# A four-stage conditional block on one core: even gathers, values through DRAM by unit, values projected from x2

## The chip, the cores and the metric

The kernel runs on 1 core of one Trainium2 chip. The metric is the time of one execution on the device in microseconds (us). TensorE is called PE, VectorE DVE, ScalarE ACT, GpSimd POOL and SyncE SP.

## What is computed

The input x has 32 sequences of 32 tokens with 256 channels. Four layers follow each other, each added to its input:

```python
x = x + einsum('bct,bcd->bdt', x, W0[cond])                     # mix of the 32 tokens, by sequence
x = x + x @ W1.T + adapter(x)                                   # rank 16, one of 8 adapters by sequence
x = x + attention(x, Wq, Wk, Wv, Wo, k_blocks, v_blocks, block_tables, kv_lens)
x = x + x @ W3[id] + b3[id]                                     # one of 16 experts by sequence
```

The attention has 8 query heads and 4 key/value heads of width 32, norms and rotations on queries and keys, and a window of 128 keys. Keys and values of the past lie in blocks of 16 rows. Each sequence first writes its 32 new keys and values into the pools at the blocks that its table names. Block tables may name one block several times, and in several sequences, so a written row can be seen through any of them.

## The kernel before

Below, x1 is the result of the first layer and x2 that of the second. Everything is float32. The sequences stand in three units of 11, 11 and 10. Each sequence sees at most 11 blocks in its window, so a unit is a tile `blkp[u]` of 121 or 110 partitions, one block each, with keys and values of 16 rows side by side. A fourth set of 96 blocks (index `NU`) holds the blocks that are written.

The order of the work is written out by hand: each engine has one instruction list, and semaphores join them. An engine that waits holds everything behind it in its list.

- **Front.** PE turns the weights, composes keys and values with layer 1 (`W1` plus the identity, times `Wk` and `Wv`), mixes the tokens (`mix_down`, L970), makes x1, projects keys and values from x1 (`project_kv`, L990) and runs layer 1 (L1003) to x2, from which it projects the queries (L1017). The composed weights let keys and values start before x2 exists.
- **Gathers.** POOL gathers table entries (L442) and then the blocks: 8 indirect DMAs (L449), each with one row of 8 KB for each of 96, 121 or 110 partitions, in the order writers, unit 0, unit 1, unit 2. ACT or DVE rearrange each from its raw place (`permute`, L562 and L809) into `blkp`. The gathers of unit 2 reuse the raw space of the writers' blocks.
- **Rows of the writes.** A chain on PE, DVE and POOL works out which written row each new row replaces: PE selects (L1182), POOL shifts (L476), DVE writes `row_i` (L900).
- **Scatter and patch.** The writers' blocks go to DRAM (L356). POOL scatters the new keys and values over them by 8 indirect DMAs (L499), the first four after the first half of keys and values is ready, the others after the second. When all have landed, three indirect DMAs (L507) fetch the blocks that were written over `blkp[0]`, `blkp[1]` and `blkp[2]`: the patches.
- **Values.** After the patch SP moves the values of each sequence from `blkp` into the shape that PE needs, 128 rows into `Vm` (L376) and 48 into `Vt` (L377), two DMAs for a sequence, 64 in all:

```python
sp.dma_start(Vm[:, b, :], by_o[u][main:main + BP, :, 1, :]).then_inc(s_v[b // B4], 16)
sp.dma_start(Vt[lo:lo + KB, b // 2, b % 2, :], by_o[u][tail:tail + BT_, :, 1, :]).then_inc(s_v[b // B4], 16)
```

- **Experts.** Then SP loads expert weights (L391, 256 KB each), 16 ahead and 16 in the loop. They lie in the space of `blkp[0]` and `blkp[2]`, so they need its keys turned and its values moved. The biases (L516, POOL) lie in `blkp[1]`.
- **Loop.** PE turns the keys (L1048) and queries, then walks over 16 pairs of sequences: scores (L1067), DVE adds the mask and takes the maximum (L933), ACT exponentiates (L680), POOL normalises (L522), PE turns the probabilities (L1079) and multiplies the values (L1102). After each group of four sequences PE projects (L1115) and runs layer 3 (L1128), and SP writes the result (L402). A group is two pairs, and there are 8 groups.

## Time and profile before

| | |
|---|---|
| median of 3 runs | 203.7 us (203.66 to 204.32) |
| the profiled execution's own time | 204.03 us |
| its span | 202.2 us, 3950 instructions |
| PE busy | 125.5 us (62%) |
| ACT busy | 88.2 us (44%) |
| DVE busy | 72.7 us (36%) |
| POOL busy | 67.9 us (34%) |
| DMA | 30.51 MB, mean 151 GB/s |

The span runs from the first to the last instruction of the profiled execution; the time around it (1.8 us) is not in the profile. Times in the rows below are us from the start of the span. The chain of waits is followed back from the last instruction: at each step to what released it. PEclk is the clock that PE was granted as a share of the full 2.4 GHz, and the DMA share is the mean busy share of the core's 16 DMA engines.

### The profile page before, as it was taken

To read this page: it belongs to the slowest core of one execution; us is meant where nothing else is said; L and a number is where in the kernel's file an instruction comes from. 1 tells how busy PE (TensorE), PEld (TensorE's weight loads), DVE (VectorE), ACT (ScalarE), POOL (GpSimd) and SP (SyncE) were. 2 spreads that over 40 slices of the span, in tenths; PEclk is the share of its full clock that TensorE was granted. 3 is DMA by queue.
4 is the path that set the end of the run, shared out by engine and by line. 5 is a ranking of instruction groups with operands and counts; after the bars stand their busy time and mean duration, and the time that the engine had idled before them with its cause. 6 is when DMAs were issued, how large, how long until landed. Compare 5 with 4: busy or idle time off the path is not lost.

```text
span 202.2 us, 3950 instructions
## 1 busy us (share of the span) xinstructions
PE 125.5 (62%) x1400; PEld 94.0 (46%) x1400; DVE 72.7 (36%) x307; ACT 88.2 (44%) x244; POOL 67.9 (34%) x83
## 2 busy tenths in 40 slices
PE   0229899994039830086689700070399999999883
PEld 0129759961037320084557500050167777677571
DVE  0794445556501775002444410000033435335211
ACT  2130392737565740045979700050027567656410
POOL 4577433170067714100025000680017425224300
PEclk9999999999556996559999975555579999999999
DMA  4937999999993692994333333444777887750000
GB/s 124 313 33 218 243 177 164 138 349 245 169 195 117 176 234 61 208 150 105 66 61 65 64 61 57 100 121 118 226 242 246 255 244 200 227 164 18 29 29 26
DMA packets 25675, 30.51 MB, mean 151 GB/s; under 512 B 6585, under 2 KB 23741, under 8 KB 24398
## 3 DMA queue, kind: packets, MB, share of 16 engines
q1 hardware_dynamic: 22392, 17.96, 34.1%
q0 software_dynamic: 2848, 11.77, 28.3%
q10 hardware_dynamic: 416, 0.54, 0.8%
q8 instruction: 11, 0.18, 0.4%
q14 instruction: 8, 0.07, 0.1%
HBM read 26.91 MB, written 4.03 MB: 153 GB/s over the span
## 4 chain that ended last, share of the span: by engine, by line
DMA 29%; SPq 25%; PE 21%; issue 10%; POOL 8%; DVE 4%; ACT 1%; POOLq 1%; DVEq 0%
DMA vt_m<-in_L_cond_v_blocks,tab_i 17%; SPq L377 13%; SPq L376 10%; DMA blkp<-wr_rows,patch_i 5%; PE bank L1067 4%; PE bank L1128 4%; PE bank L1115 3%; DMA wr_rows<-kvn_m,row_i 3%; POOL wr_rows L499 3%; PE bank L1079 3%; DMA lens_i<-in_itok_B 2%; POOL tab_i L442 2%; PE bank L1123 2%; PE bank L1102 2%; DMA blkp<-in_L_cond_W 1%
## 5 line engine op out<-in xcount | busy, mean ns | idle before, releaser
L522 POOL TENSOR_TENSOR xin_m<-xin_m,ri 128x704 f32<-128x704 f32 x16 | 21.8, 1361 | 62.2 <-DVE ri L925 62.2
L680 ACT ACTIVATE xin_m<-kvn_m,nb 128x176 f32<-128x176 f32 x64 | 27.5, 435 | 5.6 <-DVE nb L933 5.6
L690 ACT COPY x_m<-bank 128x512 f32<-128x512 f32 x16 | 9.4, 589 | 44.5 <-PE bank L1079 44.5
L1067 PE MATMUL bank<-kt_m,natQ 32*64 32x176 f32 x256 | 20.7, 331 | 4.0 <-DVE nb L933 2.7
L1079 PE MATMUL bank<-cst,xin_m 128*128 128x128 f32 x64 | 11.0, 299 | 16.8 <-POOL xin_m L522 16.6
L933 DVE CUSTOM_DVE_ANT_0 kvn_m<-bank,mask 128x176 f32<-128x176 f32 x64 | 17.5, 329 | 3.6 <-PE bank L1067 3.6
L942 DVE TENSOR_TENSOR wq_m<-bank,blkp 128x256 f32<-128x256 f32 x8 | 3.4, 425 | 42.8 <-PE bank L1128 42.8
L1017 PE MATMUL bank<-wq_m,x_m 128*128 128x256 f32 x32 | 10.2, 482 | 12.4 <-ACT x_m L605 11.1
L1067 PEld LDWEIGHTS bank<-kt_m,natQ 32*64 32x64 f32 x256 | 12.6, 136 | 10.7 <-DVE nb L933 5.3
L1048 PE MATMUL bank<-cst,blkp 121*128 121x121 f32 (+1 forms) x48 | 7.3, 317 | 15.9 <-DMA blkp<-wr_rows,patch_i 15.5
L1079 PEld LDWEIGHTS bank<-cst,xin_m 128*128 128x128 f32 x64 | 7.6, 150 | 19.7 <-POOL xin_m L522 17.8
L1128 PE MATMUL bank<-blkp,wkv_m 128*32 128x256 f32 x128 | 9.6, 416 | 9.9 <-DMA blkp<-in_L_cond_W 9.9
L1017 PEld LDWEIGHTS bank<-wq_m,x_m 128*128 128x128 f32 x32 | 7.8, 254 | 15.5 <-ACT x_m L605 11.9
L1048 PEld LDWEIGHTS bank<-cst,blkp 121*128 121x128 f32 (+1 forms) x48 | 6.3, 169 | 17.0 <-DMA blkp<-wr_rows,patch_i 16.3
L516 POOL DMA_INDIRECT blkp<-in_L_cond_b,eid_i x8 | 7.9, 986 | 18.2 <-DMA vt_m<-blkp 16.9
L869 DVE TENSOR_REDUCE ssq<-ksq 128x16 f32<-128x512 f32 x4 | 2.7, 686 | 28.4 <-ACT ksq L588 16.4
L680 ACT ACTIVATION_READ_ACCUMULATOR xin_m<-kvn_m,nb 128x1 f32 x64 | 12.3, 192 | 0.0
L612 ACT COPY kt_m<-bank 128x484 f32<-128x484 f32 (+1 forms) x12 | 5.9, 569 | 13.1 <-PE bank L1048 13.1
L990 PE MATMUL bank<-wkv_m,x_m 128*128 128x128 f32 x64 | 10.1, 280 | 0.0
L1115 PE MATMUL bank<-w_m,WoT 128*128 128x128 f32 x64 | 9.3, 288 | 1.1 <-DVE w_m L920 1.1
L1128 PEld LDWEIGHTS bank<-blkp,wkv_m 128*32 128x32 f32 x128 | 4.0, 115 | 12.4 <-DMA blkp<-in_L_cond_W 10.2
L1115 PEld LDWEIGHTS bank<-w_m,WoT 128*128 128x128 f32 x64 | 7.7, 191 | 2.9 <-issue 1.5
(192 smaller groups left out, 274.6 us busy)
## 6 DMA issues: line engine op xcount, KB each, us to landing
blkp<-in_L_cond_W SPq DMA_DIRECT2D x32, 256.0 KB, 3.4
vm_m<-blkp SPq DMA_DIRECT2D x32, 64.0 KB
wr_rows<-blkp SPq DMA_DIRECT2D x1, 1536.0 KB, 16.2
mask<-mask_rows SPq DMA_DIRECT2D x4, 352.0 KB
xin_m<-in_x SPq DMA_DIRECT2D x2, 512.0 KB
out<-wq_m SPq DMA_DIRECT2D x8, 128.0 KB, 3.1
vt_m<-blkp SPq DMA_DIRECT2D x32, 24.0 KB
mask_rows<-m SPq DMA_DIRECT2D x4, 88.0 KB
```

Source lines behind the costliest of these rows:

```text
L376: sp.dma_start(Vm[:, b, :], by_o[u][main:main + BP, :, 1, :]).then_inc(s_v[b // B4], 16)
L377: sp.dma_start(Vt[lo:lo + KB, b // 2, b % 2, :], by_o[u][tail:tail + BT_, :, 1, :]).then_inc(s_v[b // B4], 16)
L522: pool.tensor_tensor(e_, e_, ri[:, p % 2, :].unsqueeze(2).broadcast_to([P, 4, KEYS]), ALU.mult).then_inc(s_pn, 1)
L680: act.activation(pr_seq(n % 2, u, j), S[:, n % 2, u, j, :], ACT.Exp, bias=nb[:, n % 2, 2 * u + j:2 * u + j + 1], scale=-1.0, accum_out=rs[ ...
L933: dve.tensor_tensor_reduce(S[:, n % 2, u, j, :], bank[2 + (2 * n + u) % 3][:, j * KEYS:(j + 1) * KEYS], mask[:, 2 * n + j, :], -SCALE, 3e3 ...
L990: mm(o, x1T[:, kc, tile], WkvT[:, kc, w], start=(kc == 0), stop=False)
L1017: i_ = mm(o, x2T[:, kc, t * P:(t + 1) * P], WqT[:, kc, :, :].rearrange("p s c -> p (s c)"), start=(kc == 0), stop=(kc == KC - 1))
L1048: i_ = tr(bank[KT_BANK[c % 4]][:, o * P:o * P + PU[u]], by_o[u][0:PU[u], 4 * (c % 4) + o, 0, :], ident[0:PU[u], 0:PU[u]])
L1067: i_ = mm(bank[2 + i % 3][GS * T * k:GS * T * k + GS * T, j * KEYS:(j + 1) * KEYS], QT[h, b // B4, b % B4, :], KT[h, b, :], start=True, st ...
L1079: i_ = tr(bank[5 + p % 2][:, (2 * j + u) * P:(2 * j + u + 1) * P], pr_main(p % 2, u, j), ident)
L1115: i_ = mm(bank[7][:, oc * P:(oc + 1) * P], WoT[:, s, oc * P:(oc + 1) * P], oT[:, g % 2, :, s, :], start=(s == 0), stop=(s == GS - 1))
L1128: i_ = mm(o[T * j:T * j + T, :], x3T[:, g % 2, kc, T * j:T * j + T], We(b)[:, kc, :], start=False, stop=(kc == KC - 1), skip_group_check=True)
```

## The change

- All gathers of the three units, and the patches, take 128 partitions. The additional table entries are read but used by nobody; the patch index of the additional rows is set so that they fetch nothing.
- The values of a unit are stored to a DRAM tensor `v_rows` by one DMA (2048 pieces of 512 B) and read back by four (two for `Vm`, two for `Vt`; even and odd sequences apart). SP does store 0, loads 0, store 1, experts 0 to 3, loads 1, store 2, experts 4 to 7, loads 2, experts 8 to 15. The experts of a space wait for the unit's store instead of its 22 copies.
- Only keys are projected from x1 by composed weights. Values are projected from x2 by plain `Wv`, kept in a new tile `WvT`.
- The composing, and the turning of `W1`, `A1` and `B1`, stand ahead of the mixing on PE; the adapter weights are loaded ahead of x. DVE adds the identity first, and does the selection of offsets and the tables after the angles; three of the eight mixing copies are ACT's instead of four.
- Both writers' blocks are rearranged on DVE, in raw space `vt_m`, which POOL then zeroes before the gathers of unit 2 (in the raw space of unit 0). The zeroing used to stand after unit 1, ahead of the scatters.
- ACT does layer 1's copies of x2 ahead of the rearranging of unit 1, and the two copies of values only after x2.
- The scores of a pair wait once and signal once, by sequence outside and half inside.
- `dist` moves out of x2's space, so that x2 no longer waits for the masks; the first query copy does.

```diff
-            for b in range(B):
-                u = UNIT_OF[b]
-                q = WB * (b - SEQS[0] * u)
-                if q == 0:
-                    sp.wait_ge(s_patch[u], 16)
-                main, tail, lo = (q + BT_, q, KB) if b % 2 else (q, q + BP, 0)
-                sp.dma_start(Vm[:, b, :], by_o[u][main:main + BP, :, 1, :]).then_inc(s_v[b // B4], 16)
-                sp.dma_start(Vt[lo:lo + KB, b // 2, b % 2, :], by_o[u][tail:tail + BT_, :, 1, :]).then_inc(s_v[b // B4], 16)
...
-                        moved(sp, u)
+                        sp.wait_ge(s_vo[u], 16)
...
+            def values_out(u):
+                sp.wait_ge(s_patch[u], 16)
+                sp.dma_start(v_rows[u].rearrange("(p o) c -> p o c", o=BLOCK), by_o[u][:, :, 1, :]).then_inc(s_vo[u], 16)
+
+            def values_back(u):
+                sp.wait_ge(s_vo[u], 16)
+                if u == 0:
+                    sp.wait_ge(s_vz, 1)
+                    for i in ((2, 0), (2, 1)):
+                        sp.wait_ge(s_perm[i], 1)
+                b0, b1 = SEQS[0] * u, SEQS[0] * u + SEQS[u]
+                src = v_rows[u][0:PU[u] * BLOCK, :].rearrange("(b r) c -> r b c", r=KEYS)
+                for i in range(2):
+                    b = b0 + (b0 + i) % 2
+                    main, tail, lo = (KB, 0, KB) if i else (0, P, 0)
+                    sp.dma_start(Vm[:, b:b1:2, :], src[main:main + P, b - b0::2, :]).then_inc(s_v[u], 16)
+                    sp.dma_start(Vt[lo:lo + KB, b // 2:(b1 - 1 - i) // 2 + 1, i, :], src[tail:tail + KB, b - b0::2, :]).then_inc(s_v[u], 16)
...
             def load_blocks(i):
                 u, kv = i
-                n = PU[u] if u < NU else NWI
+                n = P if u < NU else NWI
...
+            pool.memset(vt_m[:, :], 0.0).then_inc(s_vz, 1)
+            for kv in range(2):
+                pool.wait_ge(s_perm[0, kv], 1)
                 load_blocks((2, kv))
...
-                pool.indirect_dma_start(out=blkp[u][0:PU[u], :], out_offset=None, in_=wr_blocks,
-                                        in_offset=bass.IndirectOffsetOnAxis(ap=patch_i[0:PU[u], u:u + 1], axis=0),
+                pool.indirect_dma_start(out=blkp[u][:, :], out_offset=None, in_=wr_blocks,
+                                        in_offset=bass.IndirectOffsetOnAxis(ap=patch_i[:, u:u + 1], axis=0),
...
             permute((0, 0))
             keep_k(0)
+            act.wait_ge(s_ids, 16)
+            act.copy(idf[:, :], ids_i[:, :]).then_inc(s_idf, 1)
             root_k(0)
...
+            def project_v(i):
+                pe.wait_ge(s_x2, 2 * i + 2)
+                for t in range(4):
+                    o = bank[3 + i][:, t * KV:t * KV + KV]
+                    tile = slice((4 * i + t) * P, (4 * i + t + 1) * P)
+                    for kc in range(KC):
+                        i_ = mm(o, x2T[:, kc, tile], WvT[:, kc, :], start=(kc == 0), stop=(kc == KC - 1))
+                i_.then_inc(s_vp, 1)
...
-                for u in range(2):
-                    i = 2 * p + u
-                    if i >= 3:
-                        pe.wait_ge(s_mx, 2 * (i - 2))
-                    for j in range(2):
-                        b = 2 * p + j
+                if p:
+                    pe.wait_ge(s_mx, 4 * p - 2)
+                for j in range(2):
+                    b = 2 * p + j
+                    for u in range(2):
```

What the change moves stands in the instruction lists. SP, before, from the mask loads to the first expert (`vm_m` is the space of `Vm`, `vt_m` of `Vt`; a name in brackets is a semaphore waited for):

```order
L364 DMA mask<-mask_rows 32x5632 x3
L376 DMA vm_m<-blkp 128x1x128 [waits blocks_permuted20,blocks_permuted21,blocks_permuted31,patched0,blocks_permuted30,v_tails_zeroed]
L377 DMA vt_m<-blkp 48x1x128
...
L390 TENSOR_LOAD ids_i [waits v_moved1,v_moved0,v_moved2,k_turned,ids_loaded]
L390 ISA x2
L391 ISA
L391 DMA blkp<-in_L_cond_W 128x2x256
```

SP, after, the same place:

```order
L362 DMA mask<-mask_rows 32x5632 x3
L382 DMA v_rows<-blkp 2048x1x128 [waits patched0,ids_loaded]
L395 DMA vm_m<-v_rows 128x6x128 [waits blocks_permuted20,blocks_permuted21,v_tails_zeroed,values_out0]
L396 DMA vt_m<-v_rows 48x6x128
L395 DMA vm_m<-v_rows 128x5x128
L396 DMA vt_m<-v_rows 48x5x128
L382 DMA v_rows<-blkp 2048x1x128 [waits patched1]
L375 TENSOR_LOAD ids_i [waits values_out0,k_turned]
L375 ISA x2
L376 ISA
L376 DMA blkp<-in_L_cond_W 128x2x256
```

Between the mask loads and the first expert 64 DMAs stood before; now 6 stand there.

ACT, before, from the root of the second key half (L576) to the copies of x2 (L605); L562 rearranges a gather, L572 copies values, L642 makes distances:

```order
L576 ACTIVATE rstdk<-ssk,eps 128x16 [waits k_sums_ready]
L572 COPY kvn_m<-bank 128x4x128 [waits v_projected]
L642 ACTIVATE x_m<-cst,mid 128x176 x4
L562 COPY blkp<-vt_m 121x4x16x32 [waits blocks_loaded10]
L572 COPY kvn_m<-bank 128x4x128 [waits v_projected]
L562 COPY blkp<-vt_m 121x4x16x32 [waits blocks_loaded11]
L647 COPY WoT<-bank 128x512 [waits wo_turned]
L605 COPY x_m<-bank 128x512 [waits token_masks_ready,layer1_done]
L605 COPY x_m<-bank 128x512 [waits layer1_done]
```

ACT, after (L587 root, L627 distances, L616 x2, L573 rearranging, L583 values):

```order
L587 ACTIVATE rstdk<-ssk,eps 128x16 [waits k_sums_ready]
L627 ACTIVATE qn_m<-cst,mid 128x176 x5
L652 COPY WoT<-bank 128x512 [waits wo_turned]
L616 COPY x_m<-bank 128x512 [waits layer1_done] x2
L573 COPY blkp<-kt_m 128x4x16x32 [waits blocks_loaded10]
L583 COPY kvn_m<-bank 128x4x128 [waits v_projected]
L616 COPY x_m<-bank 128x512 [waits layer1_done] x2
L573 COPY blkp<-kt_m 128x4x16x32 [waits blocks_loaded11]
L583 COPY kvn_m<-bank 128x4x128 [waits v_projected]
```

Both copies of values now stand behind copies of x2; before, x2 stood behind both.

PE, after, from the turning of Wo (L1195) to the second projection of values (L1005); L1017 and L1018 are layer 1, L1201 selects the rows:

```order
L1195 MATMUL bank<-cst,qn_m 128x128 [waits w1_kept,wo_permuted]
L1195 MATMUL bank<-cst,qn_m 128x128 x3
L1017 MATMUL bank<-x_m,w_m 128x512 [waits lora_kept,w1_kept]
L1017 MATMUL bank<-x_m,w_m 128x512
L1018 MATMUL bank<-xaT,BT 128x512
L1201 MATMUL bank<-wr,cst 32x16 [waits patch_index_ready,rows_valued]
L1201 MATMUL bank<-wr,cst 32x16 x2
L1017 MATMUL bank<-x_m,w_m 128x512 x2
L1018 MATMUL bank<-xaT,BT 128x512
L1005 MATMUL bank<-WvT,x_m 128x128 [waits x2_kept]
L1005 MATMUL bank<-WvT,x_m 128x128 x7
```

The row selection stood ahead of Wo and of layer 1 before; it now stands behind both, and the projection of values waits for the copies of x2.

## Rows read from the trace of the kernel before

**Rows 1.** Chain of waits, in order of time: start us, us, what.

```profile
20.23 35.09 DMA vt_m<-in_L_cond_v_blocks,tab_i
...
70.43 6.44 DMA wr_rows<-kvn_m,row_i
...
77.75 9.13 DMA blkp<-wr_rows,patch_i
86.95 0.66 SPq L376
...
136.28 0.76 SPq L377
...
145.03 1.96 PE bank L1128 x16
...
155.10 1.02 PE bank L1128 x16
...
163.19 1.02 PE bank L1128 x16
```

**Rows 2.** Timeline of PE: start us, us, line, operation, count [idle before].

```profile
42.33 1.88 PE L1003 MATMUL bank<-x_m,w_m 128*128 128x512 f32 x4
...
58.76 6.24 PE L1017 MATMUL bank<-wq_m,x_m 128*128 128x256 f32 x16 [11.12 <-ACT x_m L605]
...
114.22 1.16 PE L1115 MATMUL bank<-w_m,WoT 128*128 128x128 f32 x8
...
152.06 1.16 PE L1115 MATMUL bank<-w_m,WoT 128*128 128x128 f32 x8
...
155.03 1.09 PE L1128 MATMUL bank<-blkp,wkv_m 128*32 128x256 f32 x16
156.05 0.84 PE L1067 MATMUL bank<-kt_m,natQ 32*64 32x176 f32 x16
...
159.41 0.81 PE L1067 MATMUL bank<-kt_m,natQ 32*64 32x176 f32 x8 [0.38 <-DVE nb L933]
```

**Rows 3.** Timeline of SP's DMA queue, same columns.

```profile
4.89 2.56 SPq L343 DMA_DIRECT2D natB<-in_L_cond_Bm  x2
...
138.41 17.75 SPq L391 DMA_DIRECT2D blkp<-in_L_cond_W  x16
```

**Rows 4.** Windows: stretch, length, busy of five engines, PEclk, DMA share, GB/s.

```profile
18.00:24.00 6.00, 5.23 (x29) 4.51 (x28) 3.75 (x14) 0.89 (x3) 4.03 (x8) 1.00 1.06 269
26.00:40.00 14.00, 14.00 (x111) 12.01 (x110) 7.22 (x29) 8.93 (x16) 3.74 (x9) 1.00 1.03 160
...
78.00:86.00 8.00, 0.00 (x0) 0.00 (x0) 0.76 (x2) 0.00 (x0) 3.14 (x3) 0.50 0.77 162
...
101.00:114.00 13.00, 11.88 (x186) 8.72 (x186) 6.25 (x45) 11.19 (x46) 4.07 (x3) 1.00 0.36 63
```

**Rows 5.** Timeline of ACT, front part.

```profile
27.60 0.27 ACT L626 CAST idf<-ids_i 128x32 f32<-128x32 int32 x1
...
35.78 1.90 ACT L562 COPY blkp<-kt_m 121x2048 f32<-121x2048 f32 x1 [4.29 <-DMA kt_m<-in_L_cond_k_blocks,tab_i]
...
48.61 1.44 ACT L642 ACTIVATE x_m<-cst,mid 128x176 f32<-128x176 f32 x4
...
57.63 1.08 ACT L605 COPY x_m<-bank 128x512 f32<-128x512 f32 x2
```

**Rows 6.** Timeline of POOL, front part.

```profile
28.98 0.74 POOL L463 COPY qn_m<-natQ 128x256 f32<-128x256 f32 x2 [0.19 <-POOL eid L428]
...
39.62 0.26 POOL L476 TENSOR_TENSOR rows<-rows 32x40 f32<-32x40 f32 x1 [6.30 <-DVE rows L894]
...
57.36 3.51 POOL L490 MEMSET vt_m<- 128x4096 f32 x1 [12.32 <-ACT blkp L562]
61.04 1.09 POOL L499 DMA_INDIRECT wr_rows<-kvn_m,row_i  x1 [0.17 <-issue]
```

**Rows 7.** Timeline of DVE, the row numbers (four writes, last ends 46.10).

```profile
45.36 0.74 DVE L900 TENSOR_SCALAR row_i<-rowT 32x8 int32<-32x8 f32 x4
```

More of the change, by code:

```diff
@@ L322, in program @@
         out_rows = out.rearrange("b t d -> (b t) d").rearrange("(n p) d -> n p d", p=P)
-        def moved(engine, u):
-            for g in range(SEQS[0] * u // B4, (SEQS[0] * u + SEQS[u] - 1) // B4 + 1):
-                engine.wait_ge(s_v[g], 16 * 2 * B4)
         block = ctx.enter_context(nc.Block())
@@ L392, in expert @@
                     .then_inc(s_we[b % NE // B4], 16)
-            for b in range(NE):
+            def values_out(u):
[14 more added lines that the diff above has]
+                    sp.dma_start(Vt[lo:lo + KB, b // 2:(b1 - 1 - i) // 2 + 1, i, :], src[tail:tail + KB, b - b0::2, :]).then_inc(s_v[u], 16)
+            values_out(0)
+            values_back(0)
+            values_out(1)
+            for b in range(4):
+                expert(b)
+            values_back(1)
+            values_out(2)
+            for b in range(4, 8):
+                expert(b)
+            values_back(2)
+            for b in range(8, NE):
                 expert(b)
@@ L736, in _ @@
             dve.sem_inc(s_len, 1)
+            dve.wait_ge(s_w1, 16)
+            dve.wait_ge(s_cst, 16)
+            for oc in range(KC):
+                w_ = nat[:, oc, 0, oc * P:(oc + 1) * P]
+                tt(w_, w_, ident, ALU.add).then_inc(s_w1i, 1)
+            dve.wait_ge(s_mixg, 16)
+            step(ts(mixg[:, 0:T * T:T + 1], mixg[:, 0:T * T:T + 1], 1.0, None, ALU.add))
+            dve.transpose(xaT[0:T, :], mixg.rearrange("b (c d) -> b d c", c=T)).then_inc(s_mixt, 1)
+            dve.wait_ge(s_mixt, 1)
+            dve.wait_ge(s_mixz, 1)
+            for h, q in MIX_DVE:
+                cp(*mix_part(h, q)).then_inc(s_mix, 1)
+            dve.wait_ge(s_adp, 32)
+            step(cp(amask[:, :], adp_i[:, :]))
+            ts(amask[:, :], amask[:, :], C("adapter"), scal[:, 0:1], ALU.is_equal, ALU.mult).then_inc(s_am, 1)
+            dve.wait_ge(s_an, 1)
+            side(cp(ang[:, :, 1, :], ang[:, :, 0, :]))
+            side(ts(turns[:, :, 0, :], ang[:, :, 0, :], float(1 / (2 * np.pi)), ROUND, ALU.mult, ALU.add))
+            step(ts(turns[:, :, 1, :], ang[:, :, 0, :], float(1 / (2 * np.pi)), 0.25, ALU.mult, ALU.add))
+            step(ts(turns[:, :, 1, :], turns[:, :, 1, :], ROUND, None, ALU.add))
+            step(ts(turns[:, :, :, :], turns[:, :, :, :], ROUND, None, ALU.subtract))
+            as_rows = lambda t: t[:, :, :, :].rearrange("p n k e -> p (n k e)")
+            for c in (TWO_PI_HI, TWO_PI_MID, TWO_PI_LO):
+                step(stt(as_rows(ang), as_rows(turns), -float(c), as_rows(ang), ALU.mult, ALU.add))
+            step(ts(ang[:, :, 1, :], ang[:, :, 1, :], float(np.pi / 2), None, ALU.add))
+            ts(ang[:, :, :, :], ang[:, :, :, :], PI_SAFE, -PI_SAFE, ALU.min, ALU.max).then_inc(s_ar, 1)
             side(tt(sel[0:NWI, 0, :], slot[0:NWI, 2, :], C("wr_seq", NWI), ALU.mult))
-            dve.wait_ge(s_cst, 16)
             settle()
@@ L837, in _ @@
             rotations(1)
+            side(dve.memset(found[:, 0, :], 0.0))
             dve.wait_ge(s_tgt, 1)
@@ L844, in _ @@
             settle()
-            for u in range(NU):
-                side(ts(found[0:PU[u], 1, u:u + 1], found[0:PU[u], 0, u:u + 1], 0.0, float(NONE), ALU.is_equal, ALU.mult))
-            settle()
-            for u in range(NU):
-                side(stt(patch_i[0:PU[u], u:u + 1], found[0:PU[u], 0, u:u + 1], -1.0, found[0:PU[u], 1, u:u + 1], ALU.add, ALU.add))
-            settle()
+            step(ts(found[:, 1, :], found[:, 0, :], 0.0, float(NONE), ALU.is_equal, ALU.mult))
+            step(stt(patch_i[:, :], found[:, 0, :], -1.0, found[:, 1, :], ALU.add, ALU.add))
             dve.sem_inc(s_pidx, 1)
@@ L1134, in _ @@
             turn_square(0, nat, 2).then_inc(s_kvT, 1)
+            pe.wait_ge(s_w1i, KC)
+            pe.wait_ge(s_kvTk, 2)
+            for dc in range(KC):
+                for oc in range(KC):
+                    mm(bank[1][:, dc * D:dc * D + KV], nat[:, oc, 0, dc * P:(dc + 1) * P], WkvT[:, oc, 0:KV], start=(oc == 0), stop=(oc == KC - 1))
+            turn_square(0, nat, 0).then_inc(s_w1T, 1)
             pe.wait_ge(s_ab, 16)
@@ L1192, in _ @@
             layer1(0)
+            pe.wait_ge(s_val, 1)
+            pe.wait_ge(s_pidx, 1)
+            for w in range(NW):
+                i_ = mm(bank[7][0:B, w * BLOCK:(w + 1) * BLOCK], C("wr_sel", NWI, w * B, (w + 1) * B), wr[:, 3, 0:BLOCK], start=True, stop=True)
+            i_.then_inc(s_sel, 1)
             layer1(1)
-            project_q(0)
-            project_q(1)
+            project_v(0)
             layer1(2)
             layer1(3)
-            project_q(2)
+            project_v(1)
+            for i in range(3):
+                project_q(i)
             for c in range(4):
```

197 lines of the change are left out of this document (74 added, 123 removed).

## The prediction

> **What bounds the kernel now.** The chain of waits comes first, since the busy shares average over stages with different limits. Its last third is a steady loop, and before the loop stand one gather and one queue [rows 1]. Piece by piece: the gather issued at 20.23 lands 35.09 us later; the new rows are scattered, the last landing takes 6.44 us; the patch of unit 0 takes 9.13 us and lands at 86.95. From there to 137.04 the chain holds nothing but SP issuing the 64 small copies of values (the first and the last stand in the rows; 50.1 us, 0.78 us each). Only behind them do the experts load, and layer 3 of group 0 starts at 145.03. The chain is thus front (to 86.95), SP (58.1 us) and loop (57.1 us from 145.03 to the end of the span at 202.2).
>
> The timeline of PE says what the SP part hides [rows 2]. The loop had begun: its first output projection ran at 114.22, and in the running loop layer 3 (155.03) follows the projection (152.06) by 2.97 us. Unblocked, layer 3 of group 0 would have started at 117.2, which is 30.2 us after the patch. PE waited for experts and values, not for arithmetic.
>
> **The change part by part.**
>
> *Values by unit (the copies).* 64 issues go; 3 stores and 12 loads come, and the experts 0 to 3 stand behind the first store, the four loads of unit 0 and the second store. Durations do not exist in this trace for the new pieces, so I bound them. Issue: two loads of 1024 pieces each took SP 2.56 us [rows 3], so a store of 2048 pieces costs about 2.6 us and four loads about 3. Transfer: while 512 B pieces of values moved, the rate was 63 GB/s at a DMA share of 0.36 [rows 4], hence 63/0.36 = 175 GB/s if the engines were kept full; 1.05 MB takes 6 us at that rate and 17 us at the bare 63 GB/s. I take 175, since share 0.36 says that SP was the limit. With P the time at which patch 0 lands and some 2 us for a landing (an estimate; the experts took about 3 us in all): store 0 lands at P+10, the loads of unit 0 at P+19, store 1 at P+21, experts 0 to 3 (1.1 us of issue each: 16 in 17.75 us [rows 3]) at P+23. The first product with values came at P+22.3 and layer 3 needs its experts at P+30.2. Experts 4 to 7, behind store 2, land at about P+34 (needed at P+38), 8 to 15 at P+40 to P+47 (8 to 11 needed at P+46). All are covered, by 3 to 7 us; if that cover is gone, the excess is paid one for one. POOL's bias gathers wait for store 1 in front of the fourth normalisation: P+21 against P+24, covered too. So the 58.1 us shrink to 30.2: **27.9 us gained**.
>
> *A warm TensorE.* Layer 3 of group 0 to that of group 1 took 10.07 us, the next such step 8.09 [rows 1]: after the idle stretch PE ran at the granted 0.50, that is 1.2 GHz, which also shows as 0.50 in the wait for the patch [rows 4]. Without that stretch the step should be a normal one: **2.0 us gained**.
>
> *Scores in one group.* In steps with nothing between, PE already runs all 16 score records in 0.84 us; in the others the second half starts at 159.41 after a wait of 0.38 us for DVE [rows 2]. The new order waits for the same two reductions before all 16. Start 159.4 plus 0.8 is 160.2, and the next instruction began at 160.15. Zero.
>
> *The front (when the patch lands).* Removed from PE are the value projections from x1 with their adapter part and half of each composed product; the composing moves ahead of the mixing. This makes x1 some 5 us earlier, but three things keep that from reaching the patch. I follow the new order instruction by instruction.
> The keys of unit 0 (the third gather of blocks) landed at 35.78, where ACT stopped waiting for them [rows 5]. Gathers went at 269 GB/s while the 96-row ones moved (18 to 24 us) and at 160 GB/s in 26 to 40 us, DMA share 1.03 to 1.06 both times [rows 4]. So full engines moved 40% less with 121 rows. At 269 GB/s the keys of unit 0, 1.05 MB behind the 1.57 MB of the 96-row gathers, which I let begin at 17.5 us (an estimate), land at 27.3; unchanged, at 35.8. I take 29, near the rate of the even gathers.
> Then ACT: rearrange 1.9, two copies 1.1, ids to float 0.3 (now behind the keys; before at 27.60) gives 32.3. POOL: from the ids to the end of the Wo copies 1.85 us, 34.1 [rows 5, 6]. Behind that on POOL: the zeroing of the tails 3.5 and two gather issues at 1.3 (the eight scatters from 61.04 to 70.43 are 1.34 apart [rows 1, 6]), 40.2. PE turns Wo (0.6, estimate), runs layer 1 pass 0 (4 of its 6 records 1.88, so 2.7 us [rows 2]) and selects the rows at 37.8, in time. The row chain took 39.62 to 46.10 [rows 6, 7], 6.5 us: 46.7. The moved selection and tables on DVE are paid ahead of this and hidden by the gather.
> Now the new knot: ACT's root of the second key half needs DVE's sum, which stands behind the row chain: 47.7 with 1 us for both (estimate by the 0.5 us of a 128x512 copy). Behind it on ACT: five distances 1.8 [rows 5], Wo 0.6, two copies of x2 1.1: 51.2. Values now need x2, so PE starts their first projection here, after 10 us of idling: 16 records, 1.9 us by layer 1's columns, 3.1 by the 6.24 us of the 256-wide ones at the low clock [rows 2]; 2.6 gives 53.8. Layer 1 passes 2 and 3: 59.2. Copy of x2, rearranging, copy of values 3.0: 62.2. Scatters 5 to 8 start here, the last at 66.2. Its landing: 6.44 before, with the mask load in flight, which now is over; 3 us for an expert load; I take 4.5, 70.7. Patch: issue 0.8, then 9.13 us before with 121 rows; the DMA share meanwhile was 0.77 [rows 4], and with full engines it would be 7.0; I take 8. P = 79.5, against 86.95: **7.5 us gained**.
>
> *Rule against row.* [Rows 4] show no idle engines at 121 rows, only slower ones, so from rows alone the even gather could gain nothing or all of the 40%. The Trainium skill, "DMA: Bandwidth & Descriptors", section on why a DMA increments its semaphore by 16, says that a transfer is spread over the largest number up to 16 that divides its slowest dimension: 121 rows would use 11 engines, 128 use 16, and a row would be taken by 8 instead of 11 turns of an engine. By that page alone, the stretch from 23.3 us (the end of the 96-row gathers at 269 GB/s) to 35.8 would shrink by 8/11 to 9.1 us; the keys would land at 32.4, and the sum would be 3.4 us longer. That page's count of engines is not visible in the profile.
>
> *Sum.* The profiled execution took 204.03 us (span 202.2 and 1.8 around it); 204.03 - 27.9 - 2.0 - 7.5 = **166.6 us**. The median of the runs is 203.7, 0.3 below that execution, so the same gains from there give 166.3.
>
> **The rivals.**
> 1. *Gathers stay slow.* The keys of unit 0 land at 35.8, everything behind them shifts by 6.8, and P is 86.3: 173.4 us. For: the DMA share was already over 1.0. Against: 269 GB/s with 96 rows.
> 2. *Values come back late.* At 100 GB/s store 0 lands at P+14, and loads 0 with store 1 (2.0 MB) need 20 us more: the first product with values slips from P+22.3 to P+34, 12 us: about 178. For: patches 1 and 2, experts and values share the queue's engines. Against: the 175 GB/s above.
> 3. *The round trip through DRAM is the new bound, and the kernel is slower.* If pieces of 512 B move at the 63 GB/s that the window shows, each store or load takes 17 us; store 0, then loads 0 with store 1, loads 1 with store 2, loads 2 add up to 99, and experts 8 to 11 arrive at about P+104. From layer 3 of group 2 to the end are 57.1 - 2.0 - 16.2 = 39 us: 79.5 + 104 + 39 + 1.8 = 224. It beats the old time only if those experts come by P+83, that is above some 78 GB/s. Against: DMA share 0.36 at 63 GB/s.
> 4. *The front is faster than I make it*, for instance because the scatters land within 3 us and the patch in 6, and the passes of layer 1 run ahead of my ACT estimate: P about 70, 157 us.
>
> **How the numbers follow.** Chances: the sum with its own spread (159 to 173) 0.58; rival 1 0.16; rival 2 0.11; rival 3 0.04; rival 4 0.11. P's bounds are 74 (landing 3.4, patch 5.5, projections warm) and 89 (keys at 35.8, landing 6.4, patch 9.1), so 161 to 176 from the front alone, and 12 more from late values. The range 155 to 182 leaves out rival 3, the ends of rival 2 and the far side of rival 4, and should hold 8 in 10. A difference of 0.3% is about what a measurement of this kernel can tell from no change: only rival 3 reaches that far, so faster 0.95, same 0.01, slower 0.04.
>
> **What would show it.** Right: SP's first store within 1 us of patch 0 and 15 DMAs of values in all; layer 3 of group 0 some 30 us after patch 0, no PE gap over 5 us from then on, steps of 8.1 us from the first; gathers above 200 GB/s between 26 and 40 us; on ACT a wait for the sum of the second key half near 46, and the last scatter issue at 66. Wrong: a patch that lands outside 74 to 89, PE waiting for the values loaded back or for the expert weights by more than 3 us, or a loop step other than 8.1.

## The result, and the profile after

The changed kernel took 168.2 us (median of 4 runs, 166.62 to 169.18), the kernel before 204.0 on the same chip (4 runs, 203.66 to 205.33): a ratio of 0.821, 95% interval 0.813 to 0.829. The forecast was 166.6 us. The profiled execution took 166.62 us with a span of 164.8, against 204.03 and 202.2 before.

The span falls into the same three pieces as in the prediction:

| | before | forecast | after |
|---|---|---|---|
| front, until patch 0 lands (P) | 86.95 | 79.5 | 76.3 |
| P to layer 3 of group 0 | 58.1 | 30.2 | 32.5 |
| from there to the end | 57.1 | 55.1 | 56.0 |
| span | 202.2 | 164.8 | 164.8 |

The chain of waits of the kernel after, in order of time (start us, us, what), answers to [rows 1]:

```profile
16.13 10.43 DMA vm_m<-in_L_cond_k_blocks,tab_i
...
49.16 3.71 PE bank L1005 x16
...
66.03 2.55 DMA wr_rows<-kvn_m,row_i
69.38 6.92 DMA blkp<-wr_rows,patch_i
76.34 3.49 PE bank L1062 x16
...
107.35 4.68 DMA blkp<-in_L_cond_b,eid_i
```

SP has left the chain. The gather that begins it is the keys of unit 0, 10.4 us, and a value projection (L1005) is a link now. The timeline of PE (start us, us, line, operation, count [idle before]), to be read beside [rows 2]:

```profile
95.02 1.45 PE L1080 MATMUL bank<-kt_m,natQ 32*64 32x176 f32 x16 [0.49 <-DVE nb L940]
...
105.12 0.83 PE L1080 MATMUL bank<-kt_m,natQ 32*64 32x176 f32 x16 [1.26 <-DVE nb L940]
...
108.84 1.09 PE L1142 MATMUL bank<-blkp,wkv_m 128*32 128x256 f32 x16
...
117.34 1.09 PE L1142 MATMUL bank<-blkp,wkv_m 128*32 128x256 f32 x16
121.80 0.83 PE L1080 MATMUL bank<-kt_m,natQ 32*64 32x176 f32 x16 [1.22 <-DVE nb L940]
125.52 1.09 PE L1142 MATMUL bank<-blkp,wkv_m 128*32 128x256 f32 x16
```

Layer 3 of group 0 waits for no expert. The first step from layer 3 to layer 3 is 8.50 us and the next four are 8.18; the last two, 6.58 and 4.38, are as before. Inside the first step DVE waits for the biases of layer 3:

```profile
112.14 0.42 DVE L949 TENSOR_TENSOR wq_m<-bank,blkp 128x256 f32<-128x256 f32 x1 [3.54 <-DMA blkp<-in_L_cond_b,eid_i]
```

The timeline of SP's queue, beside [rows 3]:

```profile
76.36 0.57 SPq L382 DMA_DIRECT2D v_rows<-blkp  x1
87.39 0.38 SPq L395 DMA_DIRECT2D vm_m<-v_rows  x1
...
89.47 0.55 SPq L382 DMA_DIRECT2D v_rows<-blkp  x1
91.33 6.41 SPq L376 DMA_DIRECT2D blkp<-in_L_cond_W  x4
97.79 0.47 SPq L395 DMA_DIRECT2D vm_m<-v_rows  x1
```

Store 0 leaves at P, and the loads that wait for it go 11.0 us later (forecast 10). Windows of the kernel after (stretch, length, busy of five engines, PEclk, DMA share, GB/s), beside [rows 4]:

```profile
26.00:40.00 14.00, 11.76 (x73) 8.11 (x71) 9.56 (x26) 7.04 (x11) 7.47 (x10) 1.00 0.96 381
86.40:96.40 10.00, 7.70 (x73) 5.88 (x73) 3.34 (x20) 7.46 (x26) 1.35 (x1) 0.69 0.84 228
96.40:106.40 10.00, 8.73 (x142) 6.75 (x139) 3.92 (x28) 8.56 (x35) 6.38 (x6) 0.80 1.01 274
```

All transfers together move 381 GB/s in the stretch in which they moved 160 before. Besides the gathers, the store of the writers' blocks (`wr_rows`, 1.5 MB) is in flight in both. Last, the timelines of ACT, POOL and DVE in the front, beside [rows 5 to 7]:

```profile
26.58 1.90 ACT L573 COPY blkp<-vm_m 128x2048 f32<-128x2048 f32 x1 [3.10 <-DMA vm_m<-in_L_cond_k_blocks,tab_i]
...
45.71 0.31 ACT L587 ACTIVATE rstdk<-ssk,eps 128x16 f32<-128x16 f32 x1 [5.74 <-DVE ssk L876]
...
60.78 0.58 ACT L583 COPY kvn_m<-bank 128x512 f32<-128x512 f32 x1 [0.34 <-PE bank L1005]
```
```profile
31.33 3.50 POOL L481 MEMSET vt_m<- 128x4096 f32 x1
...
39.47 0.29 POOL L493 TENSOR_TENSOR rows<-rows 32x40 f32<-32x40 f32 x1
...
54.41 1.07 POOL L507 DMA_INDIRECT wr_rows<-kvn_m,row_i  x1 [10.51 <-ACT kvn_m L583]
```
```profile
32.11 2.75 DVE L856 TENSOR_SCALAR found<-found 128x3 f32<-128x3 f32 x1
...
44.22 0.74 DVE L907 TENSOR_SCALAR row_i<-rowT 32x8 int32<-32x8 f32 x4
```

Two things to see: POOL waited 10.5 us for the values that now come from x2, and a DVE instruction over 3 elements a partition took 2.75 us while POOL zeroed `vt_m`.

### The profile page after: what moved, and what is told of

Read it like the earlier page. It is cut to its first block, busy times and chain, and to the rows that moved or that the text cites. A ratio compares the mean times of both kernels' runs of the same rounds, so it can differ in the third digit from the quotient of the medians.

```text
span 164.8 us, 3872 instructions
## 1 busy us (share of the span) xinstructions
PE 116.0 (70%) x1384; PEld 89.3 (54%) x1384; DVE 76.2 (46%) x306; ACT 86.6 (53%) x243; POOL 67.1 (41%) x83
## 4 chain that ended last, share of the span: by engine, by line
PE 40%; DMA 17%; POOL 13%; issue 11%; ACT 8%; DVE 7%; POOLq 1%; SPq 0%; DVEq 0%
PE bank L1080 7%; DMA vm_m<-in_L_cond_k_blocks,tab_i 6%; PE bank L1092 4%; DMA blkp<-wr_rows,patch_i 4%; PE bank L1129 4%; PE bank L1062 4%; PE bank L1142 4%; PE bank L1005 4%; DMA blkp<-in_L_cond_b,eid_i 3%; PE bank L1116 3%; DMA lens_i<-in_itok_B 2%; PE bank L1137 2%; POOL tab_i L456 2%; POOL vt_m L481 2%; PE bank L1017 2%
## 5 line engine op out<-in xcount | busy, mean ns | idle before, releaser
L530 POOL TENSOR_TENSOR xin_m<-xin_m,ri 128x704 f32<-128x704 f32 x16 | 21.8, 1360 | 49.8 <-DVE ri L932 49.8
L1080 PE MATMUL bank<-kt_m,natQ 32*64 32x176 f32 x256 | 14.5, 343 | 10.0 <-DVE nb L940 9.1
L1080 PEld LDWEIGHTS bank<-kt_m,natQ 32*64 32x64 f32 x256 | 9.0, 141 | 14.4 <-issue 14.2
L1062 PEld LDWEIGHTS bank<-cst,blkp 121*128 121x128 f32 (+1 forms) x48 | 7.4, 191 | 13.4 <-DMA blkp<-wr_rows,patch_i 10.5
L507 POOL DMA_INDIRECT wr_rows<-kvn_m,row_i x8 | 8.0, 1006 | 15.2 <-ACT kvn_m L583 13.4
L1005 PE MATMUL bank<-WvT,x_m 128*128 128x128 f32 x32 | 5.8, 354 | 11.5 <-ACT x_m L616 11.5
L1005 PEld LDWEIGHTS bank<-WvT,x_m 128*128 128x128 f32 x32 | 5.3, 261 | 13.1 <-ACT x_m L616 13.1
L573 ACT COPY blkp<-vm_m 128x2048 f32<-128x2048 f32 x4 | 7.6, 1892 | 3.1 <-DMA vm_m<-in_L_cond_k_blocks,tab_i 3.1
L955 DVE TENSOR_TENSOR wkv_m<-bank,x_m 128x256 f32<-128x256 f32 x8 | 3.4, 425 | 11.9 <-PE bank L1129 11.9
L1142 PE MATMUL bank<-blkp,wkv_m 128*32 128x256 f32 x128 | 8.7, 385 | 0.0
L1116 PE MATMUL bank<-x_m,vm_m 128*32 128x64 f32 x256 | 8.7, 225 | 0.0
## 6 DMA issues: line engine op xcount, KB each, us to landing
wr_rows<-blkp SPq DMA_DIRECT2D x1, 1536.0 KB, 10.5
```

The costliest lines, as they stand in the source:

```text
L507: pool.indirect_dma_start(out=wr_rows, out_offset=bass.IndirectOffsetOnAxis(ap=row_i[:, n:n + 1], axis=0), in_=kvn[:, n, :], in_offset=Non ...
L530: pool.tensor_tensor(e_, e_, ri[:, p % 2, :].unsqueeze(2).broadcast_to([P, 4, KEYS]), ALU.mult).then_inc(s_pn, 1)
L1005: i_ = mm(o, x2T[:, kc, tile], WvT[:, kc, :], start=(kc == 0), stop=(kc == KC - 1))
L1062: i_ = tr(bank[KT_BANK[c % 4]][:, o * P:o * P + PU[u]], by_o[u][0:PU[u], 4 * (c % 4) + o, 0, :], ident[0:PU[u], 0:PU[u]])
L1080: i_ = mm(bank[2 + (2 * p + u) % 3][GS * T * k:GS * T * k + GS * T, j * KEYS:(j + 1) * KEYS], QT[h, b // B4, b % B4, :], KT[h, b, :], star ...
L1116: mm(o, Vm[:, b, v], PTA[:, p % 2, j, k // 2, c], start=True, stop=False)
```

## Experiments: the parts of the change

The runs came in three batches, each beside the kernel before: the four of this section (before 202.4 us, 11 runs), the first four of the next (203.8, 7 runs) and the last three (204.0, 6 runs). Ratios are to the kernel before on the same chip, with 95% intervals.

Each trace is of one execution, and the start of the front alone moves by 2 us between them: in the changed kernel and in five kernels below that have the same gathers up to there (scores by half, the two late zeroings and the two with x2 first), the keys of unit 0 land between 26.58 and 28.62. So a P that differs by less than 2 us shows nothing by itself; where it matters, P is counted below from the landing of the keys (49.8 us in the changed kernel, 50.4 in the kernel with scores by half, whose front is the same).

**Values by unit alone, on the kernel before.**

```diff
-                sp.dma_start(Vm[:, b, :], by_o[u][main:main + BP, :, 1, :]).then_inc(s_v[b // B4], 16)
...
+                sp.dma_start(v_rows[u][0:PU[u] * BLOCK, :].rearrange("(p o) c -> p o c", o=BLOCK), by_o[u][0:PU[u], :, 1, :]).then_inc(s_vo[u], 16)
...
-                pe.wait_ge(s_v[p // 2], 16 * 2 * B4)
+                pe.wait_ge(s_v[UNIT_OF[2 * p]], 64)
+                pe.wait_ge(s_v[UNIT_OF[2 * p + 1]], 64)
```

> The kernel before with the values by unit through DRAM and nothing else of the change. Theory (the 64 copies on SP held the experts back): patch 0 stays at 87, layer 3 of group 0 runs 30 to 33 us behind it instead of 58, the next step is warm: 204.0 - 27.9 - 2.0 = 174, up to 176 if the round trip costs as much as in the changed kernel. Rival (the change's gain is mostly the front, and unit-wise values only pay with even gathers): above 185.

Measured: 177.2 us, ratio 0.872 (0.865 to 0.878), span 176.5. PE's timeline:

```profile
87.25 3.49 PE L1060 MATMUL bank<-cst,blkp 121*128 121x121 f32 x16 [12.72 <-DMA blkp<-wr_rows,patch_i]
...
118.24 1.09 PE L1141 MATMUL bank<-blkp,wkv_m 128*32 128x256 f32 x16
...
128.45 1.09 PE L1141 MATMUL bank<-blkp,wkv_m 128*32 128x256 f32 x16 [0.46 <-DMA blkp<-in_L_cond_W]
```

From P to layer 3 it is 31.0 us against 58.1, as expected. This part carries 25.7 of the 37.4 us by which the span fell. The time is above the 174 to 176 expected, and the next step was not the short one: it took 10.2 us, although no stretch with an idle PE stands ahead of it. There DVE waited 4.83 us for the biases of layer 3, and the expert weights came 0.46 us late.

**Everything but that part.** The changed kernel, with the 64 copies put back.

```diff
-            values_out(0)
-            values_back(0)
...
+                sp.dma_start(Vm[:, b, :], by_o[u][main:main + BP, :, 1, :]).then_inc(s_v[b // B4], 16)
+                sp.dma_start(Vt[lo:lo + KB, b // 2, b % 2, :], by_o[u][tail:tail + BT_, :, 1, :]).then_inc(s_v[b // B4], 16)
```

> The changed kernel with the values moved by 64 copies as before. Theory (the parts add): patch 0 at 76.3, then 58.1 us to layer 3 of group 0, 57.1 from there, 1.8 around: 193. Rival (with the front shortened, copies and patches collide): above 197, or below 190 if the copies issue faster behind even patches.

Measured: 195.9 us, 0.967 (0.960 to 0.973), span 194.0. This is 2.9 us above the 193 expected. P is at 78.48, 2.1 us later than in the changed kernel, so most of the gain in front of it is kept; but SP's copies again hold layer 3 back, 58.0 us after P:

```profile
136.47 1.96 PE L1130 MATMUL bank<-blkp,wkv_m 128*32 128x256 f32 x16 [10.38 <-DMA blkp<-in_L_cond_W]
```

The two parts save 25.7 and 8.2 us of span by themselves and 37.4 together. They add, nearly. Of the 3.5 over, 2.4 lie in P and 2.7 behind layer 3 of group 0, above all in two long steps (10.2 and 9.0 us) of the kernel with only the values by unit; 1.6 go the other way, since there layer 3 followed P after 31.0 us and not 32.5.

**Gathers, patches and stores of 121 and 110 rows in the changed kernel.**

```diff
-                n = P if u < NU else NWI
+                n = PU[u] if u < NU else NWI
...
-                pool.indirect_dma_start(out=blkp[u][:, :], out_offset=None, in_=wr_blocks,
+                pool.indirect_dma_start(out=blkp[u][0:PU[u], :], out_offset=None, in_=wr_blocks,
```

> The changed kernel with gathers, patches and stores of 121, 121 and 110 partitions. Theory (the rate of the gathers is set by the count of partitions, and the front waits for the keys of unit 0): gathers fall from 381 to about 170 GB/s in 26 to 40 us, the keys of unit 0 land at 31 to 36 instead of 26.6, patch 0 moves by 4 to 9 us: 172 to 177. Rival (the order of ACT hides the gathers, the rate comes from the raw spaces or from the earlier start): same rate, or within 1.5 us of the changed kernel.

Measured: 180.4 us, 0.887 (0.879 to 0.895), span 178.1: 12 us more than the changed kernel, 13 by the ratios. Window, ACT and chain:

```profile
26.00:40.00 14.00, 5.10 (x43) 4.82 (x43) 4.88 (x23) 3.30 (x5) 2.17 (x6) 0.79 1.01 245
```
```profile
34.42 1.90 ACT L573 COPY blkp<-vm_m 121x2048 f32<-121x2048 f32 x1 [12.60 <-DMA vm_m<-in_L_cond_k_blocks,tab_i]
```
```profile
78.08 9.66 DMA blkp<-wr_rows,patch_i
```

The keys of unit 0 come 7.8 us later (34.42 against 26.58), the patch takes 2.7 us longer (9.66 against 6.92), and P moves by 11.4 to 87.8. So the row count alone is worth as much as the whole front gained, 10.6 us: without it, P is within 1 us of where it was before.
**Scores by half again.**

```diff
-                i_.then_inc(s_sc, 1)
+                    i_.then_inc(s_sc, 1)
...
-                    dve.wait_ge(s_sc, n + 1)
+                        dve.wait_ge(s_sc, 2 * n + u + 1)
```

> The changed kernel with the waits and the order of the scores of before. Theory (regrouping is neutral, as predicted): within 0.5 us. Rival (one wait for both halves makes PE wait 1.2 us for DVE once a group instead of 0.4, a step of 8.18 against 8.08): 0.7 to 1.5 us faster than the changed kernel.

Measured (6 runs): 169.1 us, 0.828 (0.822 to 0.834), span 167.6. In the steady loop PE's wait falls from 1.22 us to 0.39 and the step from 8.18 to 8.09:

```profile
132.93 0.81 PE L1081 MATMUL bank<-kt_m,natQ 32*64 32x176 f32 x8 [0.39 <-DVE nb L940]
136.65 1.09 PE L1143 MATMUL bank<-blkp,wkv_m 128*32 128x256 f32 x16
```

Over the four full steps that is 0.4 us, less than runs of one kernel differ. The time does not tell the two apart, the steady step does. The first step took 10.25 us here against 8.50, which is 1.75 us of the 2.8 by which this span is longer; this edit does not touch what it waited for, see the end of the next section.

## Experiments: what the front still waits for

**Zeroing of vt_m behind the row numbers.** POOL's memset moved from before the last two gathers to 44 us.

```diff
-            pool.memset(vt_m[:, :], 0.0).then_inc(s_vz, 1)
...
             pool.sem_inc(s_rowf, 1)
+            pool.memset(vt_m[:, :], 0.0).then_inc(s_vz, 1)
```

> The changed kernel with POOL's zeroing of the tails behind the row chain instead of ahead of the gathers of unit 2. Theory (the 3.5 us memset stands on the front's chain twice: it delays the gathers of unit 2, and a 3-element DVE instruction takes 2.75 us beside it and holds the sum that ACT's root waits for): that DVE instruction takes 0.3 us, the row chain starts at 36.5 instead of 39.5, patch 0 moves from 76.3 to 73.4: about 165. Rival (the DVE instruction is slow for another reason and POOL has slack): patch 0 within 1 us of 76.3.

Measured: 169.7 us, 0.839 (0.830 to 0.848): not faster. DVE and POOL tell why:

```profile
34.22 0.22 DVE L856 TENSOR_SCALAR found<-found 128x3 f32<-128x3 f32 x1
...
44.30 3.95 DVE L907 TENSOR_SCALAR row_i<-rowT 32x8 int32<-32x8 f32 x4
```
```profile
44.14 3.51 POOL L498 MEMSET vt_m<- 128x4096 f32 x1 [0.15 <-POOL rows L494]
```

The 2.75 us were due to the zeroing, as thought: without it beside them they are 0.22. But the zeroing takes the delay along: the row numbers beside it take 3.95 us in place of 0.74. In these two instructions the edit gave 2.5 us and took 3.2. P is 79.5; of the 3.2 us by which it is later, 1.9 were there when the keys landed (28.47).

**Copies of x2 ahead of the key root on ACT.**

```diff
             keep_k(1)
-            root_k(1)
...
             keep_x2(0)
             keep_x2(1)
...
+            root_k(1)
             keep_v(0)
```

> The changed kernel with ACT's first two copies of x2, Wo and the rearranging of unit 1's keys ahead of the root of the second key half, and the distances later. Theory (ACT's order, not PE, DMA or POOL, sets the front: ACT sits 5.7 us at the root while the finished x2 waits behind it): values of the second half are kept near 52 instead of 61.4, patch 0 lands at 67 to 69; ACT's query work then ends near 70 and takes back 1 to 3 us: 160 to 162. Rival (the gathers or the row chain bind right behind it): patch 0 at 73 or later.

Measured: 166.5 us, 0.813 (0.798 to 0.829), span 161.7 in the profiled execution; the interval does not part it from the changed kernel. P was to land at 67 to 69 and the time to be 160 to 162; P is 72.3. The last scatter is issued 8.4 us earlier, P comes only 4.0 earlier. The chain:

```profile
57.63 6.63 DMA wr_rows<-kvn_m,row_i
64.32 0.54 issue
65.06 7.19 DMA blkp<-wr_rows,patch_i
```

The landing takes 6.6 us in place of 2.55. The window masks, 1.4 MB which SP had started at 57.09, are in flight in those microseconds; in the changed kernel they started at 54.51, 11.5 us ahead of the last scatter. The edit itself moved them back, since it puts the last distances, from which the masks are made, behind the copies of x2.

**Both of these.**

> The zeroing late and x2 first together, on the changed kernel. Theory: the row chain ends 3 us earlier, but the last scatter then hangs on layer 1 and ACT, so the two overlap: patch 0 at 66 to 68, 157 to 161. Rival (they are one and the same delay): the same as x2 first alone within 0.5 us.

Measured: 167.9 us, 0.829 (0.817 to 0.840), span 165.3, not the 157 to 161 that the sum of the two would give. The row numbers take 3.95 us, and the last landing 8.46:

```profile
60.15 8.46 DMA wr_rows<-kvn_m,row_i
69.40 6.95 DMA blkp<-wr_rows,patch_i
```

**Values projected from x1 again**, with the composed weights, in the changed kernel. Two moves of order come with it: PE projects both halves ahead of layer 1's second half, and ACT keeps both halves ahead of the second key root, where the kernel before kept them behind it.

```diff
-                        i_ = mm(o, x2T[:, kc, tile], WvT[:, kc, :], start=(kc == 0), stop=(kc == KC - 1))
+                        mm(o, x1T[:, kc, tile], WkvT[:, kc, KV:2 * KV], start=(kc == 0), stop=False)
+                    i_ = mm(o, xaT[:, tile], BKV[:, KV:2 * KV], start=False, stop=True)
```

> The changed kernel with the values projected from x1 by composed weights again, right behind layer 1's first half, and kept by ACT ahead of the root of the second key half. Theory (projecting from x2 put layer 1 and two copies of x2 in front of the scatters and cost the front more than the 3 us of PE work it saved): last scatter issue near 54, patch 0 at 64 to 68, 159 to 163. Rival (the saved PE work is worth more, since the row selection stands on PE): patch 0 at 76 or later, 168 or more.

Measured: 162.4 us, 0.795 (0.783 to 0.806), span 158.7: faster than the change. By the ratios it is 5.4 us, and an estimate from the two intervals puts that within 3 us either way; the runs scattered from 160.5 to 164.9. How much of it is the source of the values and how much the new places on ACT and PE was not tried apart. The scatters start at 45.72, 8.7 us earlier, and P is 68.2. The landing is slow again:

```profile
55.72 4.50 DMA wr_rows<-kvn_m,row_i
61.01 7.14 DMA blkp<-wr_rows,patch_i
```

**The same with the masks early.** ACT's five distances go ahead of `keep_v`, DVE's mask ahead of the transposition of the row numbers.

```diff
+            dve.wait_ge(s_dist, NT)
+            ts(m4_own[:, :, :], dist, (WINDOW / 2) ** 2, -BIG, ALU.is_ge, ALU.mult).then_inc(s_m4, 1)
             dve.wait_ge(s_rowf, 1)
```

> The kernel whose values come from x1 again (run e7), with the window masks made and spread earlier: ScalarE's last five distances before it keeps the values, VectorE's mask built before the row numbers are transposed. Theory (the 1.4 MB of mask loads, 56.06 to 61.99 in that run, share the DMA engines with the last scatters, 52 to 56.7, and hold their landing back: 4.32 us waited behind the last issue, where the changed kernel with its masks out by 60.5 and its last scatter issued at 66.03 waited 2.23): mask loads near 50 to 56, the wait for the last landing 2 to 2.5 us, patches 1 to 2 us earlier, span 156.5 to 158. Rival 1 (the landing is the scatters' own, 512 kB in rows of 512 B, whatever else is loaded): wait 4 to 5, span 158 to 159.5. Rival 2 (the queries behind, not the patches, bound the next step): patches earlier, span unchanged.

Measured: 158.6 us, 0.776 (0.769 to 0.784), span 157.7. SP's queue and the chain:

```profile
47.16 2.92 SPq L361 DMA_DIRECT2D mask<-mask_rows  x4
```
```profile
56.18 2.40 DMA wr_rows<-kvn_m,row_i
59.38 6.93 DMA blkp<-wr_rows,patch_i
```

The landing is 2.4 us again, so the masks had held it back, and P is 66.4. The theory holds. The median moved by more (3.8 us) than P (1.8); the two were not run side by side, and their intervals touch. Counted from the keys, P came after 41.7 us there and 39.7 here. The span of the profiled execution fell by only 1.0, since its first step was longer (10.75 us against 10.41).

**Zeroing last, alone and on top of the masks.** The memset stands behind the three patches.

```diff
+            pool.memset(vt_m[:, :], 0.0).then_inc(s_vz, 1)
             pool.wait_ge(s_eidi, 1)
```

> The changed kernel with GpSimd's zeroing of vt_m (3.5 us) moved behind the patches' issue at 72. Theory (a VectorE instruction that reads one tensor and a scalar can't run beside that zeroing: found<-found took 2.75 us beside it, and 0.22 with the zeroing moved to 44, where the row numbers then took 3.95 us in place of 0.74): both short again, found 0.2 and row numbers 0.7; second patched half of unit 0 waits less; patch 0 at 74.5 to 76, span 163 to 165, unless one of the recips or copies of the query rotation (VectorE from 64 on) stalls in their place, which would show as a long instruction at 72 to 76. Rival (the 2.75 us is a wait for something else, such as the matmul before): found stays long, span 164.8.

Measured: 168.1 us, 0.819 (0.810 to 0.828): no gain, where P was to land at 74.5 to 76. It landed at 78.3, which counted from the keys (28.62) is 49.7 us, as in the changed kernel. Yet both DVE groups are short now:

```profile
36.01 0.17 DVE L856 TENSOR_SCALAR found<-found 128x3 f32<-128x3 f32 x1
...
46.09 0.74 DVE L907 TENSOR_SCALAR row_i<-rowT 32x8 int32<-32x8 f32 x4
```

What ate the gain stands in front of them in this execution: PE waited 2.35 us for DVE's `hit` and then ran part of the key projection at the low clock (1.06 us for four records in place of 0.61), so `found` started 7.4 us behind the keys and not 5.5. One trace cannot say whether the edit brings that about.

> Both edits (masks early, zeroing last) on the kernel with values from x1. If both theories hold and add: row numbers done 0.5 to 1.5 us earlier, wait for the last landing 2 to 2.5 us, patch 0 at 64.5 to 66.5 (68.2 without them), span 155 to 157. Rival (queries bound the step after the patches): patch 0 as early, span 157.5 to 158.7.

Measured: 156.4 us (155.71 to 157.6), 0.769 (0.763 to 0.776), span 154.0: the fastest of all, 11.8 us below the change in the medians. The chain:

```profile
54.86 2.41 DMA wr_rows<-kvn_m,row_i
...
58.07 6.75 DMA blkp<-wr_rows,patch_i
64.86 3.49 PE bank L1060 x16
```

P is 64.9, 1.5 us earlier than with the masks alone (37.6 us behind the keys, against 39.7). The intervals of these two overlap, so of this last step only the rows speak. And they say that P is the smaller part: the span fell by 3.7 us, and 2.6 of them are the first step, 8.18 us here and 10.75 there. Two spans alone must not be read as the worth of the late zeroing.

**What makes the first step long.** In it DVE waits for four bias gathers (L524 in the changed kernel), which POOL issues between its normalisations. Sorted by that wait, in all kernels with values by unit and scores in one group:

| kernel | wait of DVE | first step |
|---|---|---|
| zeroing late | 2.94 | 8.18 |
| masks and zeroing last | 2.97 | 8.18 |
| zeroing last | 3.15 | 8.17 |
| x2 first | 3.26 | 8.22 |
| both late zeroing and x2 first | 3.42 | 8.37 |
| changed kernel | 3.54 | 8.50 |
| values from x1 | 3.84 | 10.41 |
| masks early | 4.23 | 10.75 |
| odd gathers | 4.76 | 11.31 |

From 3.26 us on the step grows with the wait, and between 3.54 and 3.84 it jumps by 1.9 us (scores by half, with 3.80 us, took 10.25). Behind the wait PE ran at different clocks. With masks early, then in the changed kernel:

```profile
103.49 0.42 DVE L947 TENSOR_TENSOR wq_m<-bank,blkp 128x256 f32<-128x256 f32 x1 [4.23 <-DMA blkp<-in_L_cond_b,eid_i]
...
104.90:110.20 5.30, 5.22 (x66) 4.44 (x66) 1.98 (x14) 3.43 (x15) 3.90 (x4) 0.68 1.13 279
```
```profile
113.60:117.30 3.70, 3.68 (x66) 3.12 (x66) 1.92 (x14) 2.75 (x13) 2.94 (x3) 1.00 1.14 284
```

The same 66 records of PE took 5.2 us at a granted 0.68 and 3.7 at 1.00. The granted clock behind the wait is 0.67 or 0.68 in the last three kernels of the table and with scores by half, and 1.00 in the six above. So 1.5 of the 1.9 us of the jump are a slower PE, and 0.3 us more of waiting go with 2 us of span. The kernel before with the values by unit stands apart: 4.83 us, a first step of 10.21, and the clock stayed at 1.00. This is read from the traces; a kernel whose biases come early was not run.

## Why the prediction was right, and where it was off

The forecast, 166.6, is the time of the profiled execution (166.62) and 1.6 us below the median. Three misses cancel in the first: -3.2, +2.3 and +0.9 us of span. That the span comes out at 164.8, as forecast, is luck; the pieces are right to 1, 2 and 3 us.

- **Values by unit: right in mechanism, 2.3 us too good.** Forecast -27.9, in the trace 58.1 to 32.5 = -25.6, alone 58.1 to 31.0. Store 0 landed at P+11 (forecast P+10), experts 0 to 3 went out from P+15 to P+21. Nothing waited for values. In the store two misses cancel as well: SP issued it in 0.57 us, not 2.6, and the rest took 10.5 us, not 8. The step that failed is "unblocked, layer 3 would have started 30.2 us after the patch", which took over the pace of the kernel before. There PE was granted 1.00 from 97 to 107 us (P+10 to P+20), here 0.69 in the same stretch behind P, and 0.80 in the next where it was 1.00 before: part of the score groups ran at 1.2 GHz (1.45 us for 16 records in place of 0.83). And the last scores ahead of the projection waited 1.26 us for DVE, not 0.38. In the kernel before with the values by unit, the clock was 1.00 from P+10 to P+30, and layer 3 came 31.0 us behind P.
- **Warm PE: right here, by a narrow margin.** The first step went from 10.07 to 8.50 us, and PE ran at 1.00 in it; the 0.3 us above the others go with the late biases. But "without that stretch the step should be a normal one" had the path too simple. The prediction asked when the biases could leave ("P+21 against P+24, covered too") and not when they land: group 0's landed at 112.03, P+35.7, and DVE waited for them. In five other kernels without the idle stretch the first step was 10.2 to 11.3 us. By the prediction's own sign ("a loop step other than 8.1") the loop was not what it said.
- **Scores in one group: "zero" was not quite zero.** The wait in front of all 16 records is 1.22 us in the steady loop, since the first 8 no longer fill it. Four steps of 8.18 in place of 8.09 make 0.4 of the loop's +0.9, and the first of 8.50 most of the rest. I had read a pair of rows whose sum came out even and not asked what the first half had done during the wait.
- **Front: forecast 79.5, measured 76.3.** The keys of unit 0 came at 26.58 (taken 29, the row's bound 27.3), yet the chain had lost part of that by 45: DVE's `found` took 2.75 us beside the zeroing. The knot was where I had put it: ACT's key root waited 5.74 us for DVE's sum and went at 45.71 (forecast 46.7 for the row numbers and 47.7 for the root), the first value projection ran at the low clock (3.71 us; I took 2.6), the fifth scatter went at 62.20 (62.2) and the last at 66.03 (66.2). So the hit at 66 is itself a sum of misses: keys and root came 2 us early, and the projection took 1.1 longer. Behind that the terms were mis-sized: landing 2.55 (4.5) and patch 6.9 (8). These two make 3.0 of the 3.2 us.
- **Rule against row.** The rows of before let the gathers reach 269 GB/s and gave the keys at 27.3 as a bound; they landed at 26.58, and the stretch reached 381 GB/s. The Trainium skill, "DMA: Bandwidth & Descriptors", section on why a DMA increments its semaphore by 16, has 121 rows go over 11 engines and 128 over 16; the estimate by that rule was 32.4. Its direction was right: 128 rows are faster than 121. Its size was too small: 8 to 11 would be 0.73, and with only the row count changed the rate was 245 to 381, or 0.64. Whether 121 rows leave engines idle is open. The reading of [rows 4], "no idle engines at 121 rows, only slower ones", does not follow from a share of 1.03, as said at the odd gathers; I had leaned on it.
- **The rivals.** Slow gathers: refuted in the changed kernel, and made real by putting 121 rows back (180.4 us; I had priced it at 173.4). P was only 1.5 us above that price (87.8 against 86.3), although the patch was slower; the first step of 11.3 us is 3.2 more, and layer 3 came 31.5 us behind P and not 30.2. Late values and the DRAM round trip as bound: a store takes 11 us to land, not the 17 of the slow rate, and no product waits for it. The faster front was half right, through landing and patch, but not through the passes of layer 1.
- **What I never asked:** whether all parts of the change are worth having. Projecting the values from x2 put them behind the copies of x2, the row numbers and a cold PE. Undone, with the values kept ahead of the second key root, it gives 5.8 us of median, and 11.8 with the masks and the zeroing moved out of the way.

## What to carry to other kernels

Give indirect DMAs 128 partitions even where fewer rows are wanted, and look for it in GB/s at a full DMA share, since the share itself doesn't show it. When a step is taken off the path, list what else is in flight or running in the microseconds where the freed work will land: here the masks' transfer and a zeroing on another engine each took back what a move had won, and both had slack to stand elsewhere. Judge a bundle of edits by undoing each: one large gain hid a part that, with the order it forced on ACT and PE, cost some 5 us. And before two spans are compared, compare the steps that the edit does not touch: here 0.3 us more of waiting for the biases went with 2 us of span.
